# GNN layers: product with W0 ahead of the weighted edge sums, with a five-bucket sort of their own

## What is computed

```python
def _L0_gnn_ref(x, W, edge_w, src, dst):
    support = jnp.matmul(x, W)
    messages = support[src] * edge_w[:, None]
    return jax.ops.segment_sum(messages, dst, num_segments=N_NODES)

def _L0_mix_ref(x, Wq, Wk, Wv, proj):            # linear attention, elu(.)+1 features
    q_prime = _feature_map(einsum(x, Wq) @ proj); k_prime = _feature_map(einsum(x, Wk) @ proj)
    kv = einsum(k_prime, v); num = einsum(q_prime, kv)
    return num / (sum(q_prime) + EPS)

xn = _layernorm(x)
x = x + _L0_gnn_ref(xn, L0_gnn_W, edge_weight, src, dst) + _L0_mix_ref(xn, ...)
x = x + _L0_ffn_ref(_layernorm(x), ...)          # 16 experts of 98 tokens, hidden 1408
xn = _layernorm(x)
x = x + _L1_gnn_ref(xn, edge_index, edge_type_8, ...) + _L1_mix_ref(xn, ...)
x = x + _L1_ffn_ref(_layernorm(x), ...)
```

## Time and profile before

| | us |
|---|---|
| median of 3 runs (3081.08 to 3086.49) | 3084.84 |
| the profiled execution | 3088.74 |
| its span in the profile | 3086.9 |
| TensorE busy | 2763.8 (90%) |
| VectorE busy | 1873.2 (61%) |
| ScalarE busy | 1330.8 (43%) |
| GpSimd busy | 403.2 (13%) |

### The profile page before, as it was taken

How to read it: one execution, slowest core, us unless ns; L and a number is a source line. 1 busy time by engine, 2 the same in 40 slices (tenths; PEclk the granted TensorE clock), 3 DMA queues, 4 the chain that set the end, 5 groups by cost and what they waited for, 6 DMA issues and landing times.

```text
span 3086.9 us, 40078 instructions
## 1 busy us (share of the span) xinstructions
PE 2763.8 (90%) x16055; PEld 2398.9 (78%) x16055; DVE 1873.2 (61%) x2113; ACT 1330.8 (43%) x1721; POOL 403.2 (13%) x418
## 2 busy tenths in 40 slices
PE   5776798899999999999958999678999999999988
PEld 4664587777777776776648999447999999999987
DVE  6438934568878788777764555577444444444443
ACT  2314522156676676676615666456111111112221
POOL 4765500100000000000010000243200000000000
PEclk8888999999999999999979999889999999999999
DMA  5150001579999999899843111667322221113212
GB/s 147 43 146 5 1 28 64 161 256 321 335 324 326 329 335 325 327 330 326 306 131 131 46 44 42 180 230 274 127 76 70 69 76 49 52 67 128 70 58 75
DMA packets 148385, 496.24 MB, mean 161 GB/s; under 512 B 22671, under 2 KB 35343, under 8 KB 147190
## 3 DMA queue, kind: packets, MB, share of 16 engines
q1 hardware_dynamic: 116482, 429.41, 39.9%
q0 software_dynamic: 16032, 30.57, 3.8%
q10 hardware_dynamic: 15688, 33.70, 3.4%
HBM read 422.75 MB, written 70.76 MB: 160 GB/s over the span
## 4 chain that ended last, share of the span: by engine, by line
PE 70%; DVE 9%; DMA 6%; POOL 5%; issue 4%; ACT 4%; ACTq 0%; SPq 0%; DVEq 0%; POOLq 0%
PE ps L193 69%; POOL scr_edges L954 3%; DMA er<-in_wd 3%; DVE es_l L218 2%; DVE T_l L218 2%; ACT es_h L667 1%; POOL lc L1281 1%; DMA scr_adj<-acc 1%; DVE x L206 1%; ACT lh L1241 1%; DVE acc L214 1%; POOL ws_l L218 1%; ACT ll L1242 1%; DVE st L774 1%; DMA wr<-in_Wq 0%
## 5 line engine op out<-in xcount | busy, mean ns | idle before, releaser
L218 DVE TENSOR_TENSOR es_l<-er,es_h 128x1408 fp32r<-128x1408 f32 (+1 forms) x455 | 653.4, 1445 | 187.8 <-ACT es_h L667 184.9
L667 ACT ACTIVATE es_h<-er 128x1408 fp32r<-128x1408 f32 (+1 forms) x455 | 563.6, 1242 | 265.0 <-PE ps L193 191.9
L193 PE MATMUL ps<-T_h,ws_h 128*128 128x314 f32 x1856 | 431.0, 313 | 38.4 <-DVE ws_l L218 18.5
L667 ACT ACTIVATE ws_h<-wr 128x1024 fp32r<-128x1024 f32 (+1 forms) x181 | 190.8, 1055 | 554.9 <-PE ps L193 522.9
L193 PE MATMUL ps<-T_h,ws_l 128*128 128x314 f32 x1856 | 422.1, 309 | 0.0
L193 PE MATMUL ps<-T_l,ws_h 128*128 128x314 f32 x1856 | 421.1, 309 | 0.0
L193 PEld LDWEIGHTS ps<-T_h,ws_h 128*128 128x128 f32 x1856 | 311.6, 191 | 47.1 <-issue 20.1
L193 PEld LDWEIGHTS ps<-T_h,ws_l 128*128 128x128 f32 x1856 | 312.8, 191 | 0.0
L193 PEld LDWEIGHTS ps<-T_l,ws_h 128*128 128x128 f32 x1856 | 312.6, 190 | 0.0
L218 DVE TENSOR_TENSOR ws_l<-wr,ws_h 128x1024 fp32r<-128x1024 f32 x165 | 200.3, 1215 | 140.5 <-ACT ws_h L667 138.6
L193 PE MATMUL ps<-es_h,xe_h 128*98 128x512 f32 (+1 forms) x768 | 208.9, 380 | 9.9 <-DVE es_l L218 6.9
(11 more groups left out here) (394 smaller groups left out, 5216.6 us busy)
## 6 DMA issues: line engine op xcount, KB each, us to landing
er<-in_wg SPq DMA_DIRECT2D x128, 704.0 KB, 6.7
er<-in_wu SPq DMA_DIRECT2D x128, 704.0 KB, 5.8
er<-in_wd SPq DMA_DIRECT2D x176, 512.0 KB, 5.1
scr_adj<-acc SPq DMA_DIRECT2D x123, 314.0 KB, 2.9
wr<-in_rel SPq DMA_DIRECT2D x64, 512.0 KB, 3.6
wr<-in_Wqkv SPq DMA_DIRECT2D x24, 512.0 KB, 3.6
steps<-scr_adj POOLq DMA_DIRECT2D x7, 1570.0 KB, 7.8
wr<-in_gate SPq DMA_DIRECT2D x16, 512.0 KB, 3.5
```

Of the source, the lines that this page charges most:

```text
L193: return e.matmul(out, l, r, start=start, stop=stop, skip_group_check=True)
L218: return e.tensor_tensor(lo, src, hi.bitcast(F32), ALU.subtract)
L667: q.e.activation(c.hi, c.at, ACT.Copy).then_inc(*self.s("high").up(c.key))
```

## The change

- W0 is multiplied first: support = xn W0 (`t_nat` within `t_mix0`, between qf and kv), and its result is split into high and low and put where nat lay (`spread`). After the sums by edges, A is multiplied with it, tile by tile of targets, and VectorE adds the result straight to x (`t_spread`, `v_spread`). The product into T and its splitting are gone.
- The weighted sums have a sort of their own into 5 buckets (blocks of sources), each padded to 3 chunks of 128, 32 groups (NG) and 96 chunks (NW): `v_features`, `p_sort`, `widx`, `scr_wedges`. The three chunks of a group are added up in the banks, and VectorE adds once per group. `od` has five buffers, `lc`, `lh`, `ll` four; `od` of later chunks is made ahead of the addition.
- The sort into 40 buckets is moved into `v_mix0`, in six pieces between the chunks of W0, and its 85 scatters into the experts, ten after each of the first nine token loads (`p_scatter`).
- x is loaded ahead of Wk's fourth chunk instead of Wq's first; the LayerNorm's transposes stand ahead of Wk's last chunk; Wq is multiplied behind kf and split by VectorE, not GpSimd; W0's chunks come ahead of WvT's.
- The small memory is laid out anew for it (not shown); the counting of chunk offsets in the sort of 40 buckets is gone, since only the weighted sums used them.

```diff
+NG, GC = 32, 3
+NW = NG * GC
...
-                W.add((n, o), a[n][o], 1024, 0, pool=True)
-        for k in range(KD):
-            W.add(("WvT", k), a["WvT"][k * 128:(k + 1) * 128, :], 1024, 0)
+                W.add((n, o), a[n][o], 1024, 0, pool=n == "Wk")
         for h in range(2):
             for i in range(4):
                 W.add(("W0", h, i), W2(a["W0"], 2 * i, 2 * i + 2, h), 1024, 0)
+        for k in range(KD):
+            W.add(("WvT", k), a["WvT"][k * 128:(k + 1) * 128, :], 1024, 0)
...
-            if c.key == ("Wq", 0):
+            if c.key == ("Wk", 3):
...
+        end, base = self.v_ends(q, "weighted", T, 128 * GC)
+        off, at = m["off"][0:1, :], m["o2"][0:1, 0:NG]
+        ts(e, at, self.iota[0:1, 0:NG], end[0:1, 0:1], None, ALU.is_ge).then_inc(*S.up())
+        for b in range(1, T - 1):
+            q.wait_ge(S)
+            stt(e, at, self.iota[0:1, 0:NG], end[0:1, b:b + 1], at, ALU.is_ge, ALU.add).then_inc(*S.up())
+        q.wait_ge(S)
+        ts(e, off, at, float(NT), None, ALU.mult).then_inc(*S.up("off"))
+        self.v_positions(q, "weighted", 0, T, base, bk)
+        self.v_index(q, bk, w_, NW, m["widx"], "widx")
...
+    def v_sort(self, q, step):
...
+        if step == 0:
+            q.wait_ge(self.s("mix0_sums"), ("qf", 1))
+            e.memset(m["smk"][0:TP, :], 1.0).then_inc(*S.up())
+            q.wait_ge(S)
+            e.memset(m["smk"][0:TP, 0:NBK * EC:EC], 0.0).then_inc(*S.up())
+            stt(e, bk, typf, float(T), blk, ALU.mult, ALU.add).then_inc(*S.up())
+            self.v_rank(q, "related", NBK, bk, "soh", "ssc", "smk")
+        if step == 1:
+            self.ends = self.v_ends(q, "related", NBK, 128)
+        if step == 2:
+            self.v_positions(q, "related", 0, NBK // 2, self.ends[1], bk)
+        if step == 3:
+            self.v_positions(q, "related", NBK // 2, NBK, self.ends[1], blk)
+            q.wait_ge(S)
+            tt(e, bk, bk, blk, ALU.add).then_inc(*S.up())
+            self.v_index(q, bk, blk, NCH, m["idx"], "idx")
...
+            self.p_low(q, ("Wk", o))
+        q.wait_ge(self.s("sorted"), "widx")
+        q.wait_ge(self.s("sorted"), "dat")
+        q.wait_ge(self.landed("no_edges"), 1)
+        for c in range(EC):
+            to = bass.IndirectOffsetOnAxis(ap=m["widx"][0:TP, c:c + 1].bitcast(U32), axis=0)
+            e.indirect_dma_start(self.d_wedges, to, m["dat"][0:TP, 4 * c:4 * c + 4], None).then_inc(*self.landed("weighted_edges").up(c))
+        q.wait_ge(self.landed("weighted_edges"), EC - 1)
+        e.dma_start(m["se"], wedges).then_inc(*self.landed("sorted_edges").up(0))
...
+    def p_scatter(self, q, part):
+
         q.wait_ge(self.s("sorted"), "idx")
-        q.wait_ge(self.s("sorted"), "dat")
-        q.wait_ge(self.landed("no_edges"), 0)
-        for c in range(EC):
-            to = bass.IndirectOffsetOnAxis(ap=m["idx"][0:TP, c:c + 1].bitcast(U32), axis=0)
-            e.indirect_dma_start(self.d_edges, to, m["dat"][0:TP, 4 * c:4 * c + 4], None).then_inc(*self.landed("edges").up(c))
-        q.wait_ge(self.landed("edges"), EC - 1)
-        e.dma_start(m["se"], edges).then_inc(*self.landed("sorted_edges").up(0))
+        for c in range(part * 10, min(part * 10 + 10, EC)):
+            to = bass.IndirectOffsetOnAxis(ap=self.m["idx"][0:TP, c:c + 1].bitcast(U32), axis=0)
+            q.e.indirect_dma_start(self.d_edges, to, self.m["dat"][0:TP, 4 * c:4 * c + 4], None).then_inc(*self.landed("edges").up(c))
...
-        q.wait_ge(*ps.done("Wq", 3, "low"))
-        for c in range(2):
-            outs = self.t_pair(q, ("qf", c))
-            for k in range(KD):
-                w = slice(k * 256 + c * 128, k * 256 + (c + 1) * 128)
-                ins = mm3(e, outs, (m["gq_h"][:, w], m["gq_l"][:, w]), self.Tk(k), k == 0, k == KD - 1)
-            ins.then_inc(*S.up(("qf", c)))
+        ps.take("Wq", 4)
+        for o in range(KD):
+            self.t_feature(q, "Wq", o)
...
+        self.t_nat(q, "W0", 0, KD, self.Tt)
+        self.t_count(q, "related", NBK, m["ssc"])
+        self.t_nat(q, "W0", 1, KD, self.Tt)
...
+        for piece in pieces[T:]:
+            self.v_elu(q, piece)
+        for h in range(2):
+            for i in range(4):
+                self.v_low(q, ("W0", h, i))
+                if h or i == 0:
+                    self.v_sort(q, i + h)
+            for t in range(T):
+                hi, lo = self.spread(h, t)
+                q.wait_ge(*ps.done(("W0", h), t, "high"))
+                lo_of(e, lo, ps.one(ps.group["W0", h][t], TP), hi).then_inc(*ps.out(("W0", h), t, "low"))
+        q.wait_ge(self.s("product"), ("W0", 1, 3))
+        e.memset(m["Aw"][0:TP, :], 0.0).then_inc(*self.s("zeros").up("Aw"))
...
+        for g in range(NG):
+            outs = self.t_pair(q, ("weight", g))
+            for c in range(g * GC, (g + 1) * GC):
+                od = m[f"od{c % 5}"]
+                q.wait_ge(self.s("targets"), c)
+                for j, n in enumerate(("lh", "ll")):
+                    q.wait_ge(self.s("sources_weighted"), (("high", "low")[j], c))
+                    for h in range(2):
+                        ins = mm(e, outs[h][0:TP], m[f"{n}{c % 4}"][:, 0:TP], od[:, h * H:(h + 1) * H], c == g * GC and j == 0, c == g * GC + GC - 1 and j == 1)
+                ins.then_inc(*self.s("chunk").up(c))
...
+    def v_targets(self, q, c):
+        if c < 5:
+            q.wait_ge(self.s("sorted"), "idx")
+        else:
+            q.wait_ge(self.s("chunk"), c - 5)
+        ts(q.e, self.m[f"od{c % 5}"], self.iota, self.m["se"][:, 4 * c + 1:4 * c + 2], None, ALU.is_equal).then_inc(*self.s("targets").up(c))
+
...
+        for g in range(NG):
+            for c in range(g * GC + 5, min(g * GC + 8, NW)):
+                self.v_targets(q, c)
...
+            q.wait_ge(self.s("chunk"), g * GC + GC - 1)
+            if g:
+                q.wait_ge(*ps.done(("weight", g - 1)))
+            else:
+                q.wait_ge(self.s("zeros"), "Aw")
+            v = e.snap(regs[g % 8], min_val=0, max_val=(T - 1) * NT)
+            o = two(m["Aw"][0:TP, bass.ds(v, NT)])
+            tt(e, o, ps.two(ps.group["weight", g][0], slice(0, TP)), o, ALU.add).then_inc(*ps.out(("weight", g)))
...
+        for c in range(NW):
+            if c > 3:
+                q.wait_ge(self.s("sources_weighted"), ("low", c - 4))
+            e.tensor_scalar(m[f"lc{c % 4}"], self.iota[:, 0:128], se[:, c, 0:1], None, ALU.is_equal).then_inc(*self.s("sources").up(c))
...
-        self.t_aggregate(q, "agg0", lambda s: (self.s("A_low"), ("w", s)))
-        self.t_nat(q, "W0", 0, KD, self.Tt, lambda k: self.ps.done(("agg0", k), 0, "low"))
-        self.t_nat(q, "W0", 1, KD, self.Tt)
...
+            bs = ps.take(("agg", t), 2)
+            for emptied in ps.before(("agg", t)):
+                q.wait_ge(*emptied)
+            q.wait_ge(self.s("A_low"), t)
             for s in range(T):
-                q.wait_ge(*ready(s))
-                c = slice(s * D + k * 128, s * D + (k + 1) * 128)
-                R = [(m["A_h"][0:TP, s * NT + i * H:s * NT + (i + 1) * H], m["A_l"][0:TP, s * NT + i * H:s * NT + (i + 1) * H]) for i in range(2)]
-                ins = mm3(e, outs, (m["nat_h"][0:TP, c], m["nat_l"][0:TP, c]), R, s == 0, s == T - 1)
-            ins.then_inc(*self.s("aggregated").up((name, k)))
-
-    def a_aggregate(self, q, name):
-        for k in range(KD):
-            q.wait_ge(self.s("aggregated"), (name, k))
-            q.e.activation(two(self.m["T_h"][:, k * NT:(k + 1) * NT]), self.ps.two(self.ps.group[name, k][0]), ACT.Copy).then_inc(*self.ps.out((name, k), 0, "high"))
-
-    def v_aggregate(self, q, name):
-        for k in range(KD):
-            c = slice(k * NT, (k + 1) * NT)
-            q.wait_ge(*self.ps.done((name, k), 0, "high"))
-            lo_of(q.e, two(self.m["T_l"][:, c]), self.ps.two(self.ps.group[name, k][0]), two(self.m["T_h"][:, c])).then_inc(*self.ps.out((name, k), 0, "low"))
+                c = slice(s * NT + t * TP, s * NT + (t + 1) * TP)
+                ins = mm3(e, [ps.one(b, TP) for b in bs], (m["aw_h"][0:TP, c], m["aw_l"][0:TP, c]), [self.spread(h, s) for h in range(2)], s == 0, s == T - 1)
+            ins.then_inc(*self.s("aggregated").up(t))
...
+        for t in range(T):
+            for h in range(2):
+                c = slice(t * D + h * 512, t * D + (h + 1) * 512)
+                q.wait_ge(self.s("aggregated"), t)
+                q.wait_ge(*self.xd)
+                tt(e, self.x[:, c], ps.one(ps.group["agg", t][h], TP), self.x[:, c], ALU.add).then_inc(*ps.out(("agg", t), h))
+                q.wait_ge(*ps.done(("agg", t), h))
+                self.v_stats(q, 1, t, h)
...
+            if x < 9:
+                self.p_scatter(q, x)
```

515 lines of the change are left out of this document (270 added, 245 removed).

## The result

The changed kernel takes 2972.6 us (median of 4 runs, 2966.9 to 2976.3), the kernel before 3083.0 beside it: 0.9639 of it, 95% interval 0.962 to 0.9659. A second set of runs gave 0.9629 (0.961 to 0.9648). The profiled execution has a span of 2970.0 us, 116.9 less than before. The forecast was 2969 us, 115 less in the sum.

The account below looks back on a forecast made before the run. The prediction took VectorE to bound the sums and TensorE, not the scatter, to set their start after the change. Terms +10 - 67 - 60 + 2 = -115 us gave 2969 us on the median 3084.8; 8-in-10 range 2948 to 3000.

Parts of the forecast that it names:

- The stage ahead of the sums: From start to first sum: 253 us against 242.9 before, +10 us, with kf starting at 62 and TensorE setting the start.
- a chunk behind x took 14.3 us; the two about cancel: Ahead of kf: the wait for Wk's chunk behind x about cancels the 11 us saved on Wk's second chunk.
- The sort's visible part: Behind the second W0 chunk's split: first piece of the relations' sort leaves TensorE idle 10.7 us, the later pieces cost nothing.
- It is in time: First scatter, ahead of the sums: ends near 191, sorted edges ready some 55 us early; a start at 95 would also do.
- The sums: 32 groups of three chunks at 2.5 us, VectorE held at meetings of od and lc: 80 us against 147.4, -67 us.
- GpSimd makes 3 `lc` of 0.60 to 0.65 = 1.9: In the sums: GpSimd's comparisons take 1.9 us per group of three, against 2.10 us of VectorE's own time.
- rival A: In the sums: od and lc take turns in full, 3.15 us a group, 100.8 us, total 2990; chance 0.17.
- From the last addition on: Last addition to the next LayerNorm's aggregation: 41.3 us against 101.3, -60 us, of which 55.7 is W0, only moved.
- The second scatter: Relations' edges scattered in the experts, ten at a time between two token loads: +2 us, taken between 0 and 11.6.
- B: In the sums: od and lc do not meet at all, 67 us, 13 less, total 2956; chance 0.13.
- C: Ahead of the sums: all 37 us of the relations' sort stand on TensorE's path, 26 more, total 2995; chance 0.09.
- D: In the experts: scatters between token loads starve them, slower than before, 3176 at 8 us per scatter; chance 0.03.

Follow-up runs that it names:

- x_later: Changed kernel with relations' scan one W0 chunk later, Aw cleared by GpSimd, every sixth lc by VectorE, x loaded ahead of Wk's sixth chunk; 0.9551 of the kernel before.
- scan_later: Changed kernel with the scan of the relations' sort one W0 chunk later, the rest of that step where it was; 0.9613 of the kernel before.
- four_edits: Changed kernel with relations' scan one chunk later, every sixth lc by VectorE, Aw cleared by GpSimd, square root behind the fourth Wk chunk; 0.957 of the kernel before.
- w0_last: Changed kernel with aggregation and W0 back behind the sums, keeping the sums' own sort and the additions by threes; 0.9761 of the kernel before.
- after_again: The changed kernel itself, unaltered, timed and traced again beside later edits; 0.9629 of the kernel before.
- scatter_twice: Changed kernel with each of the relations' scatter writes done a second time into a spare tensor; 0.9632 of the kernel before.

## Why the prediction was right, and where not

The total is 4 us from the forecast, and part of that closeness is luck: GpSimd's pace in the sums, 2.46 us a group, happens to lie beside the 2.5 that the prediction charged to VectorE, whose own 2.23 would have made 71 us (32 x 2.23); and the errors ahead of the sums cancel.

**The stage ahead of the sums: 253 forecast, 255.3 measured,** by errors that cancel.
- kf starts at 69.3, not 62. The step that failed is "a chunk behind x took 14.3 us; the two about cancel": in the chain above Wk's chunk behind x took 20.5 us, TensorE stood still for 12.64 us, and the norm then waited 7.75 us for a square root that ScalarE had queued behind two more Wk chunks. In ten traces with this order kf starts between 65.1 and 71.4, never at 62; with x two chunks later (`x_later`) it starts at 62.6.
- Wq took 27.3 us (85.1 to 112.4), not 30. Four chunks beside an elu piece took 3.9 us each, not 4.4: VectorE's split and piece follow each other (1.2 and 2.3 us), but of ScalarE's 1.1 us only 0.45 are waited for; I had put them end to end. The other four took 2.9 us.
- The sort's visible part was 8.72 us against 10.7: the scan took 7.24 us, where the 9.26 of the earlier trace rows include a wait for GpSimd (below). kv's banks 1.74 (2.2), Aw's memset 3.51 (3.8). The two chunks behind the long gap took 16.5 us where two take 13.9 else, 2.6 more (2.3). `scan_later` and `four_edits` show that these gaps are real time.
- The scatter ended at 208, not 191: it began 7 us later, behind Wk's last chunk, and lost 9 us beside `soh` and the scan of VectorE's sort (below), so that a write took 1.8 us instead of 1.68. "It is in time" held with 43 us to spare; `w0_last` shows what it costs where it isn't covered.

**The sums: 80 forecast, 76.6 measured; the size held, the reason fell.** The prediction had VectorE stalled by 0.1 to 0.2 us at two or three meetings, 2.5 us a group. VectorE lost 0.02 to 0.03 us per `od`, and where it sets the pace itself, in the first 15 groups, a group takes 2.23. The step that failed stands just ahead: "GpSimd makes 3 `lc` of 0.60 to 0.65 = 1.9". Where `od` fills 60% of VectorE's time, `lc` takes 0.82 to 0.90, three are 2.46 and more, and that is the pace. The prediction had the evidence in hand (at 242 us `lc` was held for 0.45 us, `od` for 0.1) and charged the loss to the wrong engine. The wrong reason would have pointed the next edit at VectorE, which had time to spare, where relieving GpSimd is worth up to 9.4 us.
The Trainium skill, SBUF — State Buffer, "Who interferes with whom", says that the order of issue decides which of the two engines blocks. These rows don't say who issued first in each meeting, so they neither bear that out nor refute it; they show GpSimd with nearly all of the loss (0.60 to 0.82) and VectorE with hardly any (0.539 to 0.564). That the loser is shut out for the whole instruction, rival A's 3.15 us a group, isn't what `lc` shows on average: 2.46. Single comparisons do show it: of the 88 the shortest took 0.60 us, the median 0.82 and the longest 1.19, a whole `od` more.

**From the last addition on: 41.3 forecast, 41.6 measured,** and 43.1 in eight other traces with this same tail. Tiles of about 7.0 us, as taken from W0's chunks. The 1.5 us between the first profile and the second (`after_again`) are TensorE's clock. It waits 2.71 us at the end of the sums for A's split. In the first profile the granted clock of the next 7.6 us is 1.00, in the second it is 0.78, with 26 products in place of 33. By stretch, the second:

```profile
335.30:378.40 43.10, 36.74 (x150) 28.88 (x150) 18.87 (x28) 5.42 (x7) 0.00 (x0) 0.96 0.00 1
```

The forecast put that term at nothing without saying so, and the trace that it is compared with happens to be the one in which it was nothing.

**The second scatter: +2 forecast, +1.2 measured,** which is less than two traces of one kernel differ there (6.9 us), and nothing by `scatter_twice`.

**Rivals.** A (full turns) and B (no meeting): neither, as said; B's 67 us is what the sums take with GpSimd at rest. C (the sort's middle pieces surface): no, TensorE has no gap above 0.9 us beside them in the changed kernel. In `w0_last`, beside WvT's shorter chunks, they do surface. D: no, shown above.
